# Attention's value products on two column tiles of 64 queries, 66 columns streamed in place of 128

## The chip, the cores and the metric

The kernel runs on one core of a Trainium2 chip. The metric is the device time of the whole program in microseconds (us). The kernel before was timed three times: 4877.83, 4884.79 and 4883.42 us, median 4883.42 us. One execution was profiled; its trace has a span of 4877.6 us from the first to the last instruction.

## What is computed

Two graph attention layers over x of shape (8, 2048, 256), with an adjacency matrix of 2048 x 2048. The change is in the first layer, whose core is this (float32, four heads of 64, keys in chunks of 256):

```python
h = jnp.maximum(_layernorm(x, axis=-1), 0.0)
q = (x @ Wq.T + bq).reshape(B, N, H, Dh).transpose(0, 2, 1, 3)     # k, v alike; here x is h
scores = jnp.einsum('bhnd,bhjcd->bhnjc', q, kc) / jnp.sqrt(jnp.asarray(Dh, dtype=q.dtype))
scores = jnp.clip(scores, -10.0, 10.0)
scores = jnp.where(mask == 0, jnp.asarray(-10.0, scores.dtype), scores)
attn = jax.nn.softmax(scores, axis=-1)          # over the 256 keys of a chunk
ctx = jnp.einsum('bhnjc,bhjcd->bhnd', attn, vc) # summed over the chunks j
ctx = ctx.transpose(0, 2, 1, 3).reshape(B, N, Dout)
out = ctx @ Wo.T + bo
out = out + x
out = (out - mu) * jax.lax.rsqrt(var + EPS) * gamma + beta
```

The softmax is taken within each chunk of 256 keys, so every chunk and head has its own denominator. The second layer (additive attention over all 2048 nodes, then elu) is not touched.

## The kernel before

The first layer goes through the 8 batches in one loop; batches 1 to 6 are one loop body. A batch is cut into 4 strips of 512 queries (STRIP), and a strip into 32 steps: 8 chunks of keys (c) times 4 heads (h). So there are 8 x 4 x 32 = 1024 steps. One step does this:

- TensorE, `scores`: for each half r of the chunk (128 keys) a product of keys (stationary, 128 x 128) with 512 queries, twice (L637 and L638, the high and the low part of the queries), into one of three PSUM slots. Four matmuls of 512 columns.
- ScalarE (ACT), L785: exp over the slot, 128 x 1024.
- VectorE (DVE), L921: clips by `bound`, which carries the mask, and writes `probs` in SBUF, keys on the partitions, 512 queries along the row. That frees the slot.
- TensorE, `values`: for each quarter q of the strip (128 queries) and each half r of the chunk one product. The stationary operand is `probs` (128 keys x 128 queries); the moving operand is `v_s` (128 keys x values). The result stands in the PSUM tile `outs`, 128 queries on the partitions. The values of head h are 64 columns of `v_s` followed by a column of ones (E1 = 65 columns per head), so column 64 of the result is the softmax's denominator. The kernel streams 128 columns from there, 63 more than are read afterwards. Eight products of float32, each of which the chip executes as two weight loads and two matmuls, so 16 of each per step in the trace.
- VectorE: the reciprocal of column 64 (L927), and a scaled sum into `ctx_sum` (L941, four per step, or L935 for the first chunk).

The order is written out by hand. On TensorE, step i issues `scores(s, i)` and then `values(s, i - LAG)` with LAG = 2, and in some steps a few more products between them: transposes of the next batch's strip (L559), queries of the next strip (L587), the turned context (L598) and the output projection (L610). After the last strip of a batch come the keys (L568) and values (L579) of the next batch. VectorE handles step i - 3's result before it clips step i. A value product waits on `slot_free` (its probabilities were written) and on `ctx_scaled` (its `outs` tile was read).

Of the kernel before, what the change touches and what calls it, by code (L numbers as in the profile page):

```python
# [28 lines left out]
P = 128  # L29
B, N, F = 8, 2048, 256  # L30
H, D = 4, 64
E1 = D + 1
CHUNK = 256
NC = N // CHUNK
JC = CHUNK // P
NT = N // P
# [39 lines left out]
PROBS = 4  # L76
LAG = 2
OUTS = 2
# [79 lines left out]
class Both:  # L158

    def __init__(self, nc, ctx):  # L160
        sb = lambda name, shape: ctx.enter_context(nc.sbuf_tensor(name, shape, F32))
        self.wide_s = sb("wide_s", [P, KC * F])
        self.w_s = sb("w_s", [P, KC * WIDE])
        self.x_s = sb("x_q_s", [P, NT * 2 * E1 + 2 * IT * F])
        self.h_s = sb("h_q_s", [P, 2 * NT * 2 * E1])
        self.t_s = sb("t_o_s", [P, KC * N])
# [7 lines left out]
def layer0_block(nc, x, adj, wq_t, bq, wk_t, bk, wv_t, bv, wo_t, bo, gamma, beta, w, a, x1, mask_dram, s_dram, d_dram, both):  # L174
    with ExitStack() as ctx:
# [30 lines left out]
        x1_in = both.t_s[:, :].rearrange("p (t f) -> p t f", t=NT)  # L206
        q_near = both.x_s[:, 0:NT * 2 * E1].rearrange("p (t h e) -> p t h e", t=NT, h=2)
        q_far = both.h_s[:, 0:NT * 2 * E1].rearrange("p (t h e) -> p t h e", t=NT, h=2)
        h1_t = both.h_s[:, NT * 2 * E1:NT * 2 * E1 + KC * 2 * P].rearrange("p (c n) -> p c n", c=KC)
        sd, d_max = both.sd, both.d_max  # L210
# [6 lines left out]

        k_hl = sb("k_hl", [P, H, N], F32R)
        q_hl = sb("q_hl", [P, H, 2, STRIP], F32R)
        v_w = H * E1 + P - E1  # L220
        v_s = sb("v_s", [P, NT, v_w])
        bound = sb("bound", [P, 2, JC, STRIP])
        probs = sb("probs", [P, PROBS, JC, STRIP])
# [9 lines left out]
        outs = [ps(f"outs{k}", [P, IT, P]) for k in range(OUTS)]  # L233
# [54 lines left out]
        def used(b, kind, *name):  # L288

            place = USES[kind][name]  # L290
            skipped = 2
            if kind == FIRST:
                skipped = sum(place >= USES[kind][(gone, 0)] for gone in ("turn", "project"))
            return b * BATCH_USES + PROLOGUE_USES - skipped + place

        def spot(kind, *name):

            return slots[used(0, kind, *name) % SLOTS]

        def q_used(b, kind, s, qu):  # L300

            if s > 0:
                return used(b, kind, "q", s, qu)
            if kind == FIRST:
                return q_first(qu)
            return used(b, MIDDLE, "q", 0, qu) - BATCH_USES
# [225 lines left out]
        def _(pe):  # L532
# [15 lines left out]
            def fill(u):  # L548
                pe.wait_ge(slot_free, u + 1)

            def freed(u):
                pe.wait_ge(slot_free, u + SLOTS + 1)
# [39 lines left out]
            def turn(g, use, slot):  # L592

                pe.wait_ge(ctx_scaled, OUTS + (g + 1) * STEPS)
                fill(use)
                for c in range(KC):
                    for q in range(IT):
                        last = nc.tensor.transpose(slot[:, c, q * P:(q + 1) * P],  # L598
                                                   ctx_sum[:, q, 2 * c:2 * c + 2, :].rearrange("p h d -> p (h d)"),
                                                   ident[:, :])  # L600
                last.then_inc(slot_filled, 1)

            def project(turned, use, slot):

                fill(use)
                freed(turned)
                for q in range(IT):
                    out = slot[:, q // 2, (q % 2) * F:(q % 2 + 1) * F]
                    for c in range(KC):
                        last = nc.tensor.matmul(out, ctx_t[:, c, q * P:(q + 1) * P], wo_s[:, c, :],  # L610
                                                start=(c == 0), stop=(c == KC - 1))
                last.then_inc(slot_filled, 1)
# [12 lines left out]
            def batch(b, kind):  # L625
                first, last = kind == FIRST, kind == LAST

                def scores(s, i):
                    c, h = divmod(i, H)
                    slot = spot(kind, "step", s, i)  # L630
                    if i % 2 == 0 and i < H:
                        freed(q_used(b, kind, s, i // 2))
                        pe.wait_ge(q_copied[i // 2], (b * NS + s + 1) * 2 * 16)
                    fill(used(b, kind, "step", s, i))
                    for r in range(JC):
                        kt = k_hl[:, h, (c * JC + r) * P:(c * JC + r + 1) * P]
                        nc.tensor.matmul(slot[:, r, :], kt, q_hl[:, h, 0, :], start=True, stop=False)  # L637
                        end = nc.tensor.matmul(slot[:, r, :], kt, q_hl[:, h, 1, :], start=False, stop=True)  # L638
                    end.then_inc(slot_filled, 1)

                def values(s, i):
                    c, h = divmod(i, H)
                    freed(used(b, kind, "step", s, i))

                    pe.wait_ge(ctx_scaled, (b * NS + s) * STEPS + i + 1)
                    for q in range(IT):
                        for r in range(JC):
                            end = nc.tensor.matmul(outs[i % OUTS][:, q, :], probs[:, i % PROBS, r, q * P:(q + 1) * P],  # L648
                                                   v_s[:, c * JC + r, h * E1:h * E1 + P],
                                                   start=(r == 0), stop=(r == JC - 1))  # L650
                    end.then_inc(probs_used, 1)

                for s in range(NS):
                    has_before = s > 0 or not first
                    for i in range(STEPS + LAG):
                        if i == TURN_AT and has_before:
                            turn(b * NS + s - 1, used(b, kind, "turn", s), spot(kind, "turn", s))
                        if i == W_AT and has_before:
                            project(used(b, kind, "turn", s), used(b, kind, "project", s), spot(kind, "project", s))
                        if i < STEPS and not (i == 0 and s > 0):  # L660
                            scores(s, i)
                        if i == STEPS + LAG - 1 and s < NS - 1:
                            scores(s + 1, 0)
                        if i in t_pairs(s) and not last:
                            strip, pair = t_pairs(s)[i]
                            order = strip + 1 if strip < NS - 1 else 0
                            src = ahead if strip == NS - 1 else hs[:, tiles(strip), :]
                            transposes(src[:, 2 * pair:2 * pair + 2, :], T_USES * (b + 1) + 2 * order + pair + 1,
                                       used(b, kind, "t", strip, pair), spot(kind, "t", strip, pair))
                        if i in Q_AT and s < NS - 1:  # L670
                            qu = Q_AT.index(i)
                            queries(s + 1, qu, used(b, kind, "q", s + 1, qu), spot(kind, "q", s + 1, qu))
                        if i in T1_AT and s == NS - 1 and last:
                            pair = T1_AT.index(i)
                            transposes(ahead[:, pair % 2 * 2:pair % 2 * 2 + 2, :], T_USES * B + pair + 1,
                                       used(b, kind, "t1", pair), spot(kind, "t1", pair))
                        if i in P1_AT and s == NS - 1 and last:
                            pair = P1_AT.index(i)
                            project1(used(b, kind, "t1", pair), used(b, kind, "p1", pair), spot(kind, "p1", pair))
                        if STEPS - 1 <= i < STEPS - 1 + Q_USES:  # L680
                            qu = i - (STEPS - 1)
                            if s == NS - 1 and not last:
                                keys(0, qu, used(b, kind, "t", 0, 1), used(b, kind, "k", 0, qu), spot(kind, "k", 0, qu))
                        if i >= LAG:
                            values(s, i - LAG)
                if not last:
                    for s, hp in k_order()[H // 2:]:
                        keys(s, hp, used(b, kind, "t", s, 1), used(b, kind, "k", s, hp), spot(kind, "k", s, hp))
                    for k in range(V_USES):
                        make_values(k, used(b, kind, "v", k), spot(kind, "v", k))  # L690
                        if k in Q_AFTER_V:
                            qu = Q_AFTER_V.index(k)
                            queries(0, qu, used(b, kind, "q", 0, qu), spot(kind, "q", 0, qu))
# [1187 lines left out]
```

## Time and profile before

| | |
|---|---|
| timed runs, median | 4883.42 us (4877.83 to 4884.79) |
| span of the profiled execution | 4877.6 us |
| lowest timed run less that span | 0.2 us |
| TensorE matmuls (PE) | 4739.8 us, 97% of the span |
| weight loads (PEld, beside PE) | 4347.8 us, 89% |
| VectorE (DVE) | 4078.2 us, 84% |
| ScalarE (ACT) | 2977.2 us, 61% |
| value products L648 | 16384 matmuls, 1988.3 us busy |
| score products L637, L638 | 4096 matmuls, 1697.9 us busy |

Busy time counts the union of the records of an engine. A matmul's record runs from its start to the modelled end of its last result, so successive matmuls overlap: 16 records of 275 ns take less than 16 x 275 ns. The distance from start to start is what a matmul costs in a sequence. The first layer's steps run from 88 us to about 3376 us; the second layer fills the rest. PEld is the loading of a stationary operand into the array, and it overlaps the matmul before it.

### The profile page before, as it was taken

To read this page: it belongs to the slowest core of one execution; us is meant where nothing else is said; L and a number is where in the kernel's file an instruction comes from. 1 tells how busy PE (TensorE), PEld (TensorE's weight loads), DVE (VectorE), ACT (ScalarE), POOL (GpSimd) and SP (SyncE) were. 2 spreads that over 40 slices of the span, in tenths; PEclk is the share of its full clock that TensorE was granted. 3 is DMA by queue.
4 is the path that set the end of the run, shared out by engine and by line. 5 is a ranking of instruction groups with operands and counts; after the bars stand their busy time and mean duration, and the time that the engine had idled before them with its cause. 6 is when DMAs were issued, how large, how long until landed. Compare 5 with 4: busy or idle time off the path is not lost. (4 is left out here: it accounts for less than half of the span.)

```text
span 4877.6 us, 136121 instructions
## 1 busy us (share of the span) xinstructions
PE 4739.8 (97%) x56349; PEld 4347.8 (89%) x56349; DVE 4078.2 (84%) x9728; ACT 2977.2 (61%) x3317; POOL 738.5 (15%) x613
## 2 busy tenths in 40 slices
PE   7999999999999999999999999997899999999999
PEld 5998899898899988989888998996899999999998
DVE  5888788787788877878877887787899999999999
ACT  5444444444444444444444444443899999999998
POOL 3121121111121211211211211011000110100100
PEclk9999999999999999999999999999999999999999
DMA  5100100001010001000001000010321221221221
GB/s 113 53 18 18 31 27 19 23 18 27 19 31 18 18 23 27 27 15 27 20 17 32 27 18 18 21 36 22 105 79 31 76 79 31 76 79 31 76 66 38
DMA packets 173916, 186.82 MB, mean 38 GB/s; under 512 B 7520, under 2 KB 157408, under 8 KB 173152
## 3 DMA queue, kind: packets, MB, share of 16 engines
q1 hardware_dynamic: 166192, 159.49, 11.9%
q0 software_dynamic: 7088, 18.36, 1.6%
q8 instruction: 459, 7.52, 0.6%
q14 instruction: 177, 1.45, 0.1%
HBM read 110.43 MB, written 38.03 MB: 30 GB/s over the span
## 5 line engine op out<-in xcount | busy, mean ns | idle before, releaser
L785 ACT ACTIVATE slot<-slot,shift 128x1024 f32<-128x1024 f32 x1024 | 1113.5, 1088 | 1568.7 <-PE slot L638 1568.7
L648 PEld LDWEIGHTS outs<-v_s,probs 128*128 128x128 f32 x16384 | 1974.5, 192 | 106.3 <-issue 29.7
L648 PE MATMUL outs<-v_s,probs 128*128 128x128 f32 x16384 | 1988.3, 275 | 0.0
L921 DVE SCALAR_TENSOR_TENSOR probs<-slot,bound 128x1024 f32<-128x1024 f32 x1024 | 1250.3, 1223 | 368.9 <-ACT slot L785 365.3
L1555 ACT ACTIVATE u<-s_all,d_sign 128x1024 bf16<-128x1024 f32 x1024 | 1117.1, 1138 | 56.9 <-PE sums L1456 39.5
L637 PE MATMUL slot<-q_hl,k_hl 128*128 128x512 f32 x2048 | 895.2, 437 | 18.5 <-DVE probs L921 9.9
L638 PE MATMUL slot<-q_hl,k_hl 128*128 128x512 f32 x2048 | 802.7, 392 | 0.0
L941 DVE SCALAR_TENSOR_TENSOR ctx_sum<-outs,inv,ctx_sum 128x64 f32<-128x64 f32 x3584 | 770.0, 278 | 31.7
L1452 PE MATMUL sums<-x_mixed,u 128*128 128x130 f16 x8192 | 785.5, 219 | 3.7 <-issue 3.5
L1456 PE MATMUL sums<-x_mixed,mask 128*128 128x65 f16 x8192 | 759.4, 193 | 5.5 <-issue 5.5
L1687 DVE TENSOR_TENSOR u<-u,mask 128x1024 f16<-128x1024 bf16 x1024 | 694.3, 689 | 76.6 <-ACT u L1555 67.6
L1447 PE MATMUL sums<-x_plain,u 128*128 128x65 f16 x16384 | 607.7, 194 | 59.1 <-DVE u L1696 54.1
L1456 PEld LDWEIGHTS sums<-x_mixed,mask 128*128 128x128 f16 x8192 | 640.6, 98 | 6.7 <-issue 6.5
L1447 PEld LDWEIGHTS sums<-x_plain,u 128*128 128x128 f16 x16384 | 561.8, 98 | 70.8 <-issue 41.4
L1452 PEld LDWEIGHTS sums<-x_mixed,u 128*128 128x128 f16 x8192 | 534.4, 97 | 17.9 <-issue 4.4
L637 PEld LDWEIGHTS slot<-q_hl,k_hl 128*128 128x128 f32 x2048 | 388.2, 190 | 72.1 <-DVE probs L921 20.6
L638 PEld LDWEIGHTS slot<-q_hl,k_hl 128*128 128x128 f32 x2048 | 388.5, 190 | 44.8
L1696 DVE TENSOR_TENSOR u<-mask,u 128x1024 f16<-128x1024 f16 x512 | 354.6, 693 | 0.0
L747 ACT ACTIVATE bound<-mask,low 128x1024 f32<-128x1024 uint8 x256 | 292.0, 1141 | 0.8
L481 POOL TENSOR_TENSOR y_rstd<-y_moments,eps_s 128x4 f32<-128x4 f32 x32 | 6.4, 201 | 1504.8 <-DVE y_moments L908 1504.8
L927 DVE RECIPROCAL inv<-outs 128x4 f32<-128x4 f32 x1024 | 176.7, 173 | 52.6 <-PE outs L648 50.8
L1380 POOL TENSOR_TENSOR mean_neg<-moments,neg_one 128x4 f32<-128x4 f32 x28 | 35.3, 1261 | 1099.1 <-DVE moments L1624 1099.1
(156 smaller groups left out, 3678.5 us busy)
## 6 DMA issues: line engine op xcount, KB each, us to landing
q_hl<-q_hl SPq DMA_DIRECT2D x128, 256.0 KB, 3.7
s_all<-s_turned SPq DMA_DIRECT2D x64, 512.0 KB, 5.7
x_q_s<-in_x SPq DMA_DIRECT2D x32, 512.0 KB, 4.6
x<-y SPq DMA_DIRECT2D x32, 512.0 KB, 3.2
t_o_s<-x SPq DMA_DIRECT2D x16, 1024.0 KB, 5.5
out<-t_o_s SPq DMA_DIRECT2D x16, 1024.0 KB, 6.9
x_q_s<-x SPq DMA_DIRECT2D x28, 512.0 KB, 5.8
probs<-in_adj POOLq DMA_DIRECT2D x12, 512.0 KB, 8.4
```

What stands on the lines that cost most here:

```text
L637: nc.tensor.matmul(slot[:, r, :], kt, q_hl[:, h, 0, :], start=True, stop=False)
L638: end = nc.tensor.matmul(slot[:, r, :], kt, q_hl[:, h, 1, :], start=False, stop=True)
L648: end = nc.tensor.matmul(outs[i % OUTS][:, q, :], probs[:, i % PROBS, r, q * P:(q + 1) * P], v_s[:, c * JC + r, h * E1:h * E1 + P], start= ...
L785: nc.scalar.activation(slot[:, :, :], slot[:, :, :], ACT.Exp, bias=shift[:, 0:1], scale=SCALE).then_inc(act_done, 1)
L921: nc.vector.scalar_tensor_tensor(probs[:, i % PROBS, :, :], spot(kind, "step", s, i)[:, :, :], P_LOW, bound[:, (i // H) % 2, :, :], ALU.ma ...
L941: op = nc.vector.scalar_tensor_tensor(ctx_sum[:, q, h, :], outs[i % OUTS][:, q, 0:D], inv[:, i % 2, q:q + 1], ctx_sum[:, q, h, :], ALU.mul ...
L1447: last = nc.tensor.matmul(group[:, side * E1:(side + 1) * E1], left, x_plain[:, h, j // 2, part, :], start=(j == 0 and t % PER_BANK == 0 a ...
L1452: nc.tensor.matmul(group[:, :], u[:, n % RING, cols], x_mixed[:, h, j // 2, 2 * part:2 * part + 2, :].rearrange("p k e -> p (k e)"), start ...
L1456: last = nc.tensor.matmul(group[:, E1:SUM_W], mask16[:, j, i0 + t * P:i0 + (t + 1) * P], x_mixed[:, h, j // 2, 4 + part, :], start=False, ...
L1555: nc.scalar.activation(cond[:, n % RING, :], s_all[:, m % HALVES, :], ACT.Relu, bias=d_sign[:, j, h:h + 1], scale=SIGN_SCALE).then_inc(con ...
L1687: nc.vector.tensor_tensor(u[:, n % RING, :], cond[:, n % RING, :], mask16[:, j, first:first + HALF], ALU.min).then_inc(u_made, 1)
L1696: nc.vector.tensor_tensor(u2[:, n // 2 % RESTS, :], mask16[:, j, first:first + HALF], u[:, n % RING, :], ALU.subtract).then_inc(u2_ready, 1)
```

## The change

Each value product over 128 queries becomes two over 64 queries. The first writes partitions 0 to 63 of `outs`, the second partitions 64 to 127; in the built program they have a tile size of 128 x 64, at column position 0 and at column position 64 of the array, where all else around them has 128 x 128. Each streams 66 columns of `v_s` (V_COLS: 64 values, the ones, and one more column that is not read). The padding of `v_s` shrinks with it, from 323 to 261 columns per tile of keys. Nothing else is changed; VectorE reads the same places of `outs`.

```diff
+V_COLS = E1 + 1
...
-        v_w = H * E1 + P - E1
+        v_w = H * E1 + V_COLS - E1
         v_s = sb("v_s", [P, NT, v_w])
...
                     for q in range(IT):
                         for r in range(JC):
-                            end = nc.tensor.matmul(outs[i % OUTS][:, q, :], probs[:, i % PROBS, r, q * P:(q + 1) * P],
-                                                   v_s[:, c * JC + r, h * E1:h * E1 + P],
-                                                   start=(r == 0), stop=(r == JC - 1))
+                            for g in range(2):
+                                rows_of = slice(g * D, (g + 1) * D)
+                                end = nc.tensor.matmul(outs[i % OUTS][rows_of, q, 0:V_COLS],
+                                                       probs[:, i % PROBS, r, q * P + g * D:q * P + (g + 1) * D],
+                                                       v_s[:, c * JC + r, h * E1:h * E1 + V_COLS],
+                                                       start=(r == 0), stop=(r == JC - 1))
                     end.then_inc(probs_used, 1)
```

On TensorE, in the first strip, this is what stands in the instruction order of the kernel before. The names are the tiles written and read, and "128x128" is the stationary operand's columns by the streamed ones:

```order
L648 MATMUL outs<-v_s,probs 128x128 [waits ctx_scaled,slot_free]
L648 MATMUL outs<-v_s,probs 128x128 x7
L637 MATMUL slot<-q_hl,k_hl 128x512 [waits slot_free]
L638 MATMUL slot<-q_hl,k_hl 128x512
L637 MATMUL slot<-q_hl,k_hl 128x512
L638 MATMUL slot<-q_hl,k_hl 128x512
L648 MATMUL outs<-v_s,probs 128x128 [waits ctx_scaled,slot_free]
L648 MATMUL outs<-v_s,probs 128x128 x7
```

And this stands there in the changed kernel, whose lines after L217 are one higher and whose value products are L651:

```order
L651 MATMUL outs<-v_s,probs 64x66 [waits ctx_scaled,slot_free]
L651 MATMUL outs<-v_s,probs 64x66 x15
L638 MATMUL slot<-q_hl,k_hl 128x512 [waits slot_free]
L639 MATMUL slot<-q_hl,k_hl 128x512
L638 MATMUL slot<-q_hl,k_hl 128x512
L639 MATMUL slot<-q_hl,k_hl 128x512
L651 MATMUL outs<-v_s,probs 64x66 [waits ctx_scaled,slot_free]
L651 MATMUL outs<-v_s,probs 64x66 x15
```

Eight products of a step became sixteen (so 32 weight loads and 32 matmuls at execution); the score products, the waits and their places are the same. The order on the other engines is as before.

## Rows read from the trace of the kernel before

**Rows 1.** The page: busy times, and the granted clock in 40 slices.
```profile
PE 4739.8 (97%) x56349; PEld 4347.8 (89%) x56349; DVE 4078.2 (84%) x9728; ACT 2977.2 (61%) x3317; POOL 738.5 (15%) x613
PEclk9999999999999999999999999999999999999999
```

**Rows 2.** Busy by stretch: length, PE, PEld, DVE, ACT, POOL, clock, DMA.
```profile
30.00:40.00 10.00, 5.26 (x33) 5.23 (x34) 7.87 (x11) 2.18 (x3) 5.87 (x8) 0.69 0.73 138
...
1834.80:1930.90 96.10, 95.78 (x684) 87.30 (x682) 78.62 (x211) 46.15 (x44) 19.26 (x15) 1.00 0.09 23
...
1740.40:2154.80 414.40, 410.70 (x2816) 367.34 (x2816) 333.72 (x876) 195.29 (x192) 77.02 (x60) 1.00 0.08 23
```

**Rows 3.** Waits in batch 4, 1740.4 to 2154.8 us: in total, times, longest.
```profile
ACT slot L785 <- PE slot L638: 196.7, 127, 5.1
...
DVE probs L921 <- ACT slot L785: 44.8, 88, 3.2
```

**Rows 4.** Timeline of matmuls in one step: start us, length us, what.
```profile
2000.54 1.95 PE L648 MATMUL outs<-v_s,probs 128*128 128x128 f32 x16
2002.24 0.48 PE L637 MATMUL slot<-q_hl,k_hl 128*128 128x512 f32 x1
2002.56 0.40 PE L638 MATMUL slot<-q_hl,k_hl 128*128 128x512 f32 x1
2002.79 0.39 PE L637 MATMUL slot<-q_hl,k_hl 128*128 128x512 f32 x1
2003.03 0.39 PE L638 MATMUL slot<-q_hl,k_hl 128*128 128x512 f32 x1
2003.25 0.27 PE L648 MATMUL outs<-v_s,probs 128*128 128x128 f32 x1
```

**Rows 5.** Timeline of weight loads in the same step.
```profile
2000.32 1.98 PEld L648 LDWEIGHTS outs<-v_s,probs 128*128 128x128 f32 x16
2002.22 0.19 PEld L637 LDWEIGHTS slot<-q_hl,k_hl 128*128 128x128 f32 x1
2002.33 0.19 PEld L638 LDWEIGHTS slot<-q_hl,k_hl 128*128 128x128 f32 x1
```

**Rows 6.** Groups of matmuls by shape: busy us, mean ns.
```profile
L648 PE MATMUL outs<-v_s,probs 128*128 128x128 f32 x16384 | 1988.3, 275 | 0.0
...
L587 PE MATMUL slot<-t_o_s,wide_s 128*128 128x512 f32 x256 | 120.3, 592 | 0.0
...
L579 PE MATMUL slot<-wv_s,t_o_s 128*128 128x256 f32 x512 | 115.1, 379 | 0.0
```

**Rows 7.** Groups of weight loads by shape.
```profile
L648 PEld LDWEIGHTS outs<-v_s,probs 128*128 128x128 f32 x16384 | 1974.5, 192 | 106.3 <-issue 29.7 <-DVE ctx_sum L941 2.9
...
L598 PEld LDWEIGHTS slot<-ident,ctx_sum 128*128 128x128 f32 x256 | 28.0, 141 | 19.8 <-issue 13.5 <-DVE ctx_sum L941 5.4
...
L1423 PEld LDWEIGHTS pro<-ident,sd 128*16 128x16 f32 x28 | 2.5, 90 | 0.0
...
L719 PEld LDWEIGHTS slot<-ident,sd 128*64 128x64 f32 x1 | 0.1, 113 | 0.0
```

**Rows 8.** Timeline of matmuls in layer two, around one 16-column stationary operand.
```profile
3485.83 0.23 PE L1456 MATMUL sums<-x_mixed,mask 128*128 128x65 f16 x2
3485.90 0.27 PE L1423 MATMUL pro<-ident,sd 128*16 128x128 f32 x1
3486.01 0.48 PE L1447 MATMUL sums<-x_plain,u 128*128 128x65 f16 x10
```

**Rows 9.** Groups on VectorE in batch 4.
```profile
L921 DVE SCALAR_TENSOR_TENSOR probs<-slot,bound 128x1024 f32<-128x1024 f32 x128 | 156.3, 1223 | 45.3 <-ACT slot L785 44.8 <-issue 0.3
L941 DVE SCALAR_TENSOR_TENSOR ctx_sum<-outs,inv,ctx_sum 128x64 f32<-128x64 f32 x448 | 96.2, 278 | 4.0
L927 DVE RECIPROCAL inv<-outs 128x4 f32<-128x4 f32 x128 | 22.1, 173 | 6.0 <-PE outs L648 5.8
```

## The prediction

> **What bounds the kernel now.** I read the page's busy times first: PE is busy for 97% of the span, VectorE for 84%, at a clock of nine tenths or more of full speed in all slices [rows 1]. That does not say which of the two ends last, so I took the first layer apart by stretches. In one strip of 96.10 us PE is busy for 95.78 us and VectorE for 78.62 us; in a whole batch of 414.40 us it is 410.70 and 333.72 us [rows 2]. The waits agree: ScalarE waits 196.7 us of the batch for score products, VectorE 44.8 us for exp [rows 3], and TensorE waits for nearly nothing. So the first layer goes at the pace of TensorE, and every nanosecond added to its steps is added to the time, 1024 times. A nanosecond taken away counts only until VectorE is the slower one.
>
> Then one step. The value products start at 2000.54 and the next step's at 2003.25, so a step takes 2.71 us [rows 4]. Sixteen value matmuls span 1.95 us with the last one's 275 ns [rows 4, 6], so they start every (1950 - 275) / 15 = 111.7 ns. What limits that? Two things that cost the same. Streaming: 512 columns last 592 ns and 256 last 379 ns [rows 6], so a float32 column streams in 213 / 256 = 0.832 ns and 128 take 106.5 ns. Loading: a load of 16 columns lasts 90 ns, one of 64 lasts 113 and one of 128 lasts 141 [rows 7]; that is 0.455 ns a column on a fixed 83 ns, for transposes. The value products' own load of 128 float32 columns lasts 192 ns [rows 7], so (192 - 83) / 128 = 0.85 ns a column, 109 ns in all. The order of the two is a lock step: the score product's load begins at 2002.22, when the last value matmul has begun, and the next load begins at 2002.33 [rows 5], 110 ns on, when the product that used the first could begin. One load runs under one matmul, and about 5 ns are lost at each change.
>
> **The change part by part.** Removed per step: 16 matmuls of 128 columns and 16 loads of 128. Added: 32 of 66 columns and 32 loads of 64. Streaming falls not by half but grows: 32 x 66 = 2112 columns for 16 x 128 = 2048. Loading stays: 32 x 64 is 2048 columns too. So halving the stream gives nothing unless the two column tiles work at the same time; that is the whole question.
>
> - The pitch of one half, if matmuls come one after another: 66 x 0.832 = 54.9 ns of streaming, 64 x 0.85 = 54.4 ns of loading under it, and the 5.2 ns of today's pitch (111.7 less 106.5) for the change of hands: 60.1 ns.
> - The end of the run of values: the next score product loads 128 columns, which take 109 ns. Today a 106.5 ns matmul covers that load. After the change the last value matmul streams for 54.9 ns, so from its start to the score product's pass 111.7 ns, not 60.1. The score load has lost half its cover.
> - Sum for a step: before 16 x 111.7 = 1787 ns. After 31 x 60.1 + 111.7 = 1975 ns. That is 188 ns more, and 1024 x 0.188 = 192 us.
> - The start of the run is free: the first value load, now 54.4 ns, lies under a score product that takes 230 ns to the next start [rows 4].
> - VectorE, ScalarE and POOL do what they did. Their slack covers 188 ns a step, since VectorE is idle for (96.10 - 78.62) / 32 = 546 ns of one [rows 2]. The smaller fill of v_s with ones is at the start, while the first loads of x are on their way; I cost it at nothing, and it was one instruction.
> - The clock: PE stays as busy as it was, so I leave it at full speed. The row in which it was not, 30 to 40 us at 0.69 of full clock, has PE busy for 5.26 us of 10 [rows 2].
>
> No row of before shows two column tiles in turn. The bounds for the pitch of a half: above, load and stream laid end to end with the change of hands, 54.4 + 54.9 + 5.2 = 114.5 ns, a step of 32 x 114.5 = 3664 ns, +1.88 us a step. Below, both tiles wholly at once, 60.1 ns for two halves, 30 ns each, -0.77 us a step, of which VectorE lets only a part through (below). I take 60.1 because the nearest row, the lock step of today's value products, shows that each load waits for the matmul before it to start and each matmul for its load. If that holds across tiles, loads alone make it 54.4 + 5.2 = 59.6 ns, even if the streams could overlap.
>
> A change of the array's tiling. In the second layer the transposition L1423 has a stationary operand of 16 columns, which the built program places on a tile of 128 x 32, between neighbours of 128 x 128. It starts at 3485.90 and its follower at 3486.01 [rows 8]: 110 ns, which is what its 128 columns need to stream (106.5). The matmul before it is no further away either: two of 65 columns start from 3485.83 on. So going there and back costs nothing to be seen, 28 times. I cost the 2048 changes of the new kernel at nothing. The Trainium skill's page "TensorEngine Tiling (Array Packing)", section "Tiling Modes", says the opposite: changing the mode drains TensorE. The trace does not bear that out for these 28; by the rule there would be two drains in every step, the third rival below.
>
> The sum against the profiled execution: its span of 4877.6 us and some 0.2 us around it, plus 192, is 5070 us. The median of the three timed runs lies 5.6 us above that execution, so against the median it is 5075 us, which I take.
>
> **The rivals.**
>
> First, the tiles work side by side. Then the second half of one product loads and streams beside the first half, matmuls still starting in program order; of four passes (two a half) two adjacent ones overlap, so 16 x 60.1 = 0.96 us for the values. PE would need 0.96 + 0.05 (the bare score load) + 0.92 for the scores, 1.93 us a step, and VectorE is the bound. Its three groups take (156.3 + 96.2 + 22.1) / 128 = 2.15 us a step [rows 9]. For a whole batch: 414.40 - 4 x 96.10 = 30 us are projections on PE and stay. In the other 384 us VectorE works for about 4 x 78.62 = 314, so at most 70 us go, 560 in all (4318) [rows 2]. Some waits come back, as VectorE now has a chain PE, ScalarE, VectorE that must be always ready; I take 55 us a batch, 440 in all: 4440 us, 4390 to 4520. For it: different tiles share no weights and no result partitions, so nothing in the data forbids it. Against: in no row does a load begin ahead of the start of the matmul before it. The Trainium skill's "TensorEngine Tiling (Array Packing)", section "Key Properties" under "Tiling Modes", says that different tiles can run loads and matmuls in parallel; no run so far shows that. What could spoil it is the clock, if PE is idle for a fifth of each step; the only loaded stretch with such a drop had PE idle for half.
>
> Second, nearly no change. The halves alternate between tiles, so the 5.2 ns of handing over vanish under the other tile's stream, and only the loads count: 32 x 54.4 + 54.6 = 1795 ns, 8 ns more than now, +8 us. With 1 ns less or more for a half this is 32 ns a step, 33 us. 4850 to 4930 us, middle 4891.
>
> Third, on the far side: TensorE empties at each change of tiling. A matmul's record of 275 ns less 106.5 ns of streaming leaves 168 ns until its last result is out [rows 6]; twice a step that is 336 ns, 344 us over 1024 steps, on top of 192: 5419 us. It decides once a drain costs more than the 20 ns that would be visible. Rows 8 speak against it, but with one tile position only, and never with the second tile at column 64. The end-to-end bound (+1.88 us a step, 6800 us) belongs here too and has nothing for it but that the case was never seen.
>
> **How the numbers follow.** Forecast 0.40 (5030 to 5100), side by side 0.35, nearly no change 0.13, drains or worse 0.12. A change of 0.2%, 10 us, is about what a measurement of this kernel can tell. Faster: 0.35 and 0.05 of the second rival, 0.40. Within 0.2%: 0.04 of it. Slower: 0.40 + 0.04 + 0.12 = 0.56. The likeliest is 5075 us, alone 5030 to 5100. The cases lie on both sides, so the range is wide: 4400 (the first rival without its last tenth) to 5110, leaving out the drains and the tails.
>
> **What would show it.** A step's length, 2.71 us now, should read 2.90 in the timeline. The 32 value matmuls should start every 60 ns, their run from the first one to the score product's real start last 1.98 us, of which the last 112 ns are one load. The group's mean should be 275 - 62 x 0.832 = 223 ns, the load's 137. VectorE's share should fall, its wait for exp grow. If the halves' starts come in close pairs (4 to 30 ns apart and then a gap), the tiles overlap, the step is near 2.2 us and TensorE's waits for `slot_free` and `ctx_scaled` appear: I am wrong on the sign. If a gap of more than 100 ns stands between the last 512-column matmul and the first value matmul, beyond its 230 ns, it is the drain.

## The result and the profile after

The changed kernel takes 4494.94 us (median of four runs, 4492.85 to 4499.48), against 4883.88 us before in the same comparison: a ratio of 0.9207, with a 95% interval of 0.9194 to 0.922. It is 389 us faster where I had forecast 192 us slower. The first rival, two tiles that work side by side, is what happened, and at 4440 us it promised somewhat more than came.

The page of the changed kernel, with the lines that answer to [rows 1, 6, 7]:

```profile
PE 4246.6 (95%) x72733; PEld 3492.7 (78%) x72733; DVE 4024.7 (90%) x9728; ACT 2977.8 (66%) x3317; POOL 714.7 (16%) x613
...
PEclk9999999999999999999999999989999999999999
...
L651 PEld LDWEIGHTS outs<-v_s,probs 128*64 128x64 f32 x32768 | 1042.2, 137 | 450.5 <-issue 271.3
...
L651 PE MATMUL outs<-v_s,probs 128*64 128x66 f32 x32768 | 1179.5, 225 | 62.7 <-DVE ctx_sum L945 58.1
```

One value matmul lasts 225 ns and one load 137 ns, as predicted (223 and 137): what a half costs alone was right. But 32768 of them make 1179.5 us of busy time where 16384 made 1988.3 [rows 6]. The timeline of one step shows how (start us, length us, what), first the matmuls, then the weight loads:

```profile
1660.23 0.40 PE L638 MATMUL slot<-q_hl,k_hl 128*128 128x512 f32 x1
1660.46 0.40 PE L639 MATMUL slot<-q_hl,k_hl 128*128 128x512 f32 x1
1660.79 1.15 PE L651 MATMUL outs<-v_s,probs 128*64 128x66 f32 x32
1661.87 0.50 PE L638 MATMUL slot<-q_hl,k_hl 128*128 128x512 f32 x1
```

```profile
1660.78 1.01 PEld L651 LDWEIGHTS outs<-v_s,probs 128*64 128x64 f32 x32 [0.37 <-DVE ctx_sum L945]
1661.87 0.19 PEld L638 LDWEIGHTS slot<-q_hl,k_hl 128*128 128x128 f32 x1
1661.98 0.19 PEld L639 LDWEIGHTS slot<-q_hl,k_hl 128*128 128x128 f32 x1
```

The 32 matmuls span 1.15 us where 16 took 1.95 us [rows 4]. Cut down to 15 ns at the start of the run, the same timeline has two of them:

```profile
1660.79 0.28 PE L651 MATMUL outs<-v_s,probs 128*64 128x66 f32 x2
```

Two matmuls within 0.28 us, of which each alone is 0.27 us long: they start 7 ns apart. Their loads start 7 ns apart too. The last record is 0.222 us long, and the first one begins with a load that nothing covers (0.05 us). Without these two the 16 pairs have a pitch of (1.15 - 0.27) / 15 = 0.059 us by these rounded figures, and 58.3 ns by the starts in the trace. That is about the pitch I expected of one half; it is that of two.

The second thing to see is what stands around the run. Before, the first load of the values began 3 ns after the last score product had started. Now it begins 0.32 us after (1660.46 to 1660.78), although score products in a row start every 0.23 us: some 0.095 us are lost. At the end the last value matmul starts at 1661.72 (1660.79 + 1.15 - 0.22), and the score product's load follows 0.15 us later, where 66 columns stream for 0.055 us: again 0.095 us are lost. The trace puts the first of these gaps down to VectorE (`ctx_sum`); the experiments show that this is the wrong name in a plain step.

The step's median fell from 2.709 to 2.214 us, and TensorE is still back to back in it: 0.93 (scores) + 0.93 (values) + 0.35 (two stalls of 0.095 us, and the loads that they lay bare, about 0.10 us for a score product and 0.05 us for a value product). By stretches, with the columns of [rows 2], a strip and a batch:

```profile
1630.90:1714.70 83.80, 80.33 (x1192) 60.22 (x1192) 76.75 (x211) 46.16 (x44) 19.25 (x15) 1.00 0.10 27
1547.30:1911.60 364.30, 348.31 (x4864) 259.25 (x4865) 326.77 (x877) 195.34 (x192) 77.05 (x60) 1.00 0.10 27
```

A strip went from 96.10 to 83.80 us, 12.3 us less. 32 plain steps would give 32 x 0.495 = 15.8 us. Most of the rest is in steps in which VectorE has a side job: its work is 76.75 us of the 83.80, and such steps last 2.3 to 3.0 us. Of the 1023 distances between steps in the first layer, 598 are under 2.25 us. Another part is at the turn of a strip: its last two steps take 10.97 us together where they took 10.65 (means over 18 strips). There TensorE now waits for a DMA that brings the next strip's queries, 2.9 us in the whole kernel before and 35.9 us now:

```profile
L637 PE MATMUL slot<-q_hl,k_hl 128*128 128x512 f32 x2048 | 895.2, 437 | 18.5 <-DVE probs L921 9.9 <-DVE v_s L865 4.8 <-DMA q_hl<-q_hl 2.9
L638 PE MATMUL slot<-q_hl,k_hl 128*128 128x512 f32 x2048 | 919.7, 449 | 59.1 <-DMA q_hl<-q_hl 35.9
```

The first line is of the kernel before, the second of the changed one; the last figures are the idle time of TensorE before these products, and what ended it.

### The profile page after: what moved, and what is told of

The parts are those of the page before. It is cut to its first block and busy times, and to the rows that moved or that the text cites. A ratio compares the mean times of both kernels' runs of the same rounds, so it can differ in the third digit from the quotient of the medians.

```text
span 4491.0 us, 168889 instructions
## 1 busy us (share of the span) xinstructions
PE 4246.6 (95%) x72733; PEld 3492.7 (78%) x72733; DVE 4024.7 (90%) x9728; ACT 2977.8 (66%) x3317; POOL 714.7 (16%) x613
## 5 line engine op out<-in xcount | busy, mean ns | idle before, releaser
L651 PEld LDWEIGHTS outs<-v_s,probs 128*64 128x64 f32 x32768 | 1042.2, 137 | 450.5 <-issue 271.3
L651 PE MATMUL outs<-v_s,probs 128*64 128x66 f32 x32768 | 1179.5, 225 | 62.7 <-DVE ctx_sum L945 58.1
L638 PE MATMUL slot<-q_hl,k_hl 128*128 128x512 f32 x2048 | 919.7, 449 | 59.1 <-DMA q_hl<-q_hl 35.9
L639 PE MATMUL slot<-q_hl,k_hl 128*128 128x512 f32 x2048 | 812.6, 397 | 0.0
L1460 PE MATMUL sums<-x_mixed,mask 128*128 128x65 f16 x8192 | 759.2, 193 | 4.6 <-issue 4.5
L1460 PEld LDWEIGHTS sums<-x_mixed,mask 128*128 128x128 f16 x8192 | 640.6, 98 | 5.9 <-issue 5.9
L1384 POOL TENSOR_TENSOR mean_neg<-moments,neg_one 128x4 f32<-128x4 f32 x28 | 21.7, 774 | 1123.2 <-DVE moments L1628 1123.2
```

Of the source, the lines that this page charges most:

```text
L651: end = nc.tensor.matmul(outs[i % OUTS][rows_of, q, 0:V_COLS], probs[:, i % PROBS, r, q * P + g * D:q * P + (g + 1) * D], v_s[:, c * JC + ...
L1460: last = nc.tensor.matmul(group[:, E1:SUM_W], mask16[:, j, i0 + t * P:i0 + (t + 1) * P], x_mixed[:, h, j // 2, 4 + part, :], start=False, ...
```

## The experiments

All start from the changed kernel; the ratios are to the kernel before, which ran beside them.

**e1_untiled66: is it just the narrower stream?**

```diff
-                            for g in range(2):
-                                rows_of = slice(g * D, (g + 1) * D)
-                                end = nc.tensor.matmul(outs[i % OUTS][rows_of, q, 0:V_COLS], ...
+                            end = nc.tensor.matmul(outs[i % OUTS][:, q, 0:V_COLS], probs[:, i % PROBS, r, q * P:(q + 1) * P],
...
```

> The value products stay on the whole array (128 queries stationary, 16 matmuls and 16 loads a step) and stream 66 columns. Theory A (the two column tiles work side by side, and today's pitch is held up by the weight load as much as by the stream): the loads of 128 float32 columns take 109 ns each, so the pitch stays 110 to 112 ns and the time stays at 4870 to 4890 us. Theory B (the gain of the change is just the narrower stream; loads are not a bound): the pitch falls to about 60 ns, the step to 1.9 to 2.2 us and the time to 4350 to 4500 us.

4891.94 us, ratio 1.0023 (1.0012 to 1.0033). From its timeline:

```profile
1662.43 0.39 PE L639 MATMUL slot<-q_hl,k_hl 128*128 128x512 f32 x1
1662.66 1.89 PE L649 MATMUL outs<-v_s,probs 128*128 128x66 f32 x16
1664.36 0.48 PE L638 MATMUL slot<-q_hl,k_hl 128*128 128x512 f32 x1
```

Half of the stream taken away, and sixteen matmuls still take 1.89 us. The load of 128 columns (192 ns long, by the prediction's estimate 109 ns of occupation) holds the pitch by itself: value matmuls start every 111.7 ns here and in the kernel before alike. Theory A holds, and B falls. The small loss fits the step of the prediction on lost cover: the score product's load now begins 54 ns after the last value matmul, which covers only half of it; a step is 2.716 us.

**e2_tiled128: two tiles, wide streams**

```diff
-V_COLS = E1 + 1
+V_COLS = P
```

> Two column tiles of 64 queries as in the change, but each streams 128 columns, so 4096 columns a step in place of 2112. Theory A (side by side): the starts come in pairs 7 ns apart, a pair every 110 to 112 ns as with one matmul of before, and the step is that of before plus the two stalls of about 148 ns at the changes between the score and the value products: 2.71 + 0.30 = 3.0 us, 5180 us. Theory C (the tiles only take turns, and the change gained by something else, such as the smaller loads): the streams add up, 32 x 111.7 = 3.57 us for the values, step 4.5 us, 6700 us.

5183.98 us, ratio 1.0623 (1.0605 to 1.0641); expected 5180.

```profile
1661.58 0.39 PE L639 MATMUL slot<-q_hl,k_hl 128*128 128x512 f32 x1
1661.89 1.97 PE L651 MATMUL outs<-v_s,probs 128*64 128x128 f32 x32
```

32 matmuls of 128 columns take as long as 16 did before (1.97 and 1.95 us). A pair starts every 109.2 ns, where 128 columns need 106.5. So streams on different column tiles overlap fully, and the narrow stream and the two tiles are each worth nothing alone: the first leaves the load as the bound, the second the stream. Together they halve the run. The difference from the kernel before, 303 us, is 1024 times the 0.30 us of the two stalls.

**e3_blocked: one tile after the other**

```diff
-                    for q in range(IT):
-                        for r in range(JC):
-                            for g in range(2):
+                    for g in range(2):
+                        for q in range(IT):
+                            for r in range(JC):
```

> The same 32 matmuls a step as the change, in another order: all 16 on the tile of queries 0 to 63 first, then all 16 on the other tile. Theory A with starts in program order: a matmul can run beside another only if its neighbour in the order is on the other tile, so nothing overlaps; the pitch is the 60 ns that I predicted for one after another, the values take 1.92 us, and the step is 0.93 + 1.92 + 0.05 + 0.30 = 3.2 us, 5350 us. Rival (each tile has a queue of its own that runs ahead): like the change, 4495 us.

5109.54 us, ratio 1.0473 (1.0456 to 1.049); expected 5350 or 4495.

```profile
1900.51 0.39 PE L639 MATMUL slot<-q_hl,k_hl 128*128 128x512 f32 x1
1900.83 1.90 PE L651 MATMUL outs<-v_s,probs 128*64 128x66 f32 x32
1902.66 0.50 PE L638 MATMUL slot<-q_hl,k_hl 128*128 128x512 f32 x1
```

The same instructions in another order lose the overlap: 1.90 us for the run. My number was too high for two reasons. On one tile the pitch is 58.3 ns, not 60. And the theory's "nothing overlaps" was too strict: in the middle of each run three matmuls start 1 to 6 ns after another, so some of the other tile's start while the first tile's last ones are still to come, and about 0.18 us of the run overlap (31 x 58.3 = 1.81 us, against 1.90 - 0.27 = 1.63). So a few matmuls can be passed over, not sixteen: neighbours in the order should be on different tiles. This is also the closest measurement of my forecast's assumption, and of its sign. That its time lies near my 5075 us is in part luck: it has 0.30 us of stalls a step that I had left out, and the overlap and the shorter pitch take most of that back.

**e4_tile0_only: is the second tile free?**

```diff
-                            for g in range(2):
+                            for g in range(2 if first and s == 0 and i < OUTS else 1):
```

> Leaves out the value products of queries 64 to 127 of each 128 (all but those of the first two steps), so half of the value products' work is gone; all else stays. Theory A: the other tile's work ran for free beside this one's, so the pitch stays at 58 ns for 16 matmuls, the run at 0.93 us and the time at 4495 us. Rival (the tiles share the load path or issue, and a pair's 58 ns are the sum of two parts): the pitch falls towards 30 ns and the run to 0.5 us; the step then goes to what VectorE needs, 2.15 us, about 4430 us. It also tells whether the stalls of about 148 ns at both ends of the run need the second tile at column 64: if yes, the first matmul of the run starts 230 ns after the last score product and not 326 ns plus a load.

4502.77 us, ratio 0.9224 (0.9208 to 0.9239).

```profile
1662.01 0.40 PE L639 MATMUL slot<-q_hl,k_hl 128*128 128x512 f32 x1
1662.33 1.15 PE L651 MATMUL outs<-v_s,probs 128*64 128x66 f32 x16
1663.41 0.50 PE L638 MATMUL slot<-q_hl,k_hl 128*128 128x512 f32 x1
```

Sixteen matmuls take the 1.15 us of thirty-two. The second tile's work is free, and the stalls are there without it.

**e5_pairs and e6_more_switches: are the gaps stalls of the tiling or waits for VectorE?**

e5 issues two steps' scores, then two steps' values:

```diff
-                        if i >= LAG:
+                        if i >= STEPS:
+                            values(s, i - LAG)
+                        elif i % 2 and i > LAG:
+                            values(s, i - LAG - 1)
                             values(s, i - LAG)
```

> The changed kernel, with TensorE's order in pairs: the score products of steps i and i+1, then the value products of steps i-2 and i-1, so half as many changes between the whole array and the 64-column tiles (steps after the last score product stay as they were). Theory D (each change empties the array and costs about 148 ns to the next real start, two per step): PE needs 2.07 us a step in place of 2.21, below VectorE's 2.15 us, so the step goes to about 2.15 to 2.18 us and the time to 4430 to 4470 us, and two of three long starts of 325 and 150 ns become starts at the normal pitch. Rival (the gaps at the changes are waits for ctx_sum or for the slots, which pairs don't shorten): 4490 us or more.

e6 splits both functions in two and alternates the parts:

```diff
...
+                        split = LAG <= i < STEPS
+                        if split:
+                            scores(s, i, 0)
+                            values(s, i - LAG, 0)
+                            scores(s, i, 1)
...
+                            values(s, i - LAG, 1 if split else None)
```

> The changed kernel with twice the changes of tiling and the same products: in steps 2 to 31 of a strip the order is scores of half r=0, half of the values, scores of r=1, the other half of the values. Theory D: 2 more changes of 148 ns in 30 of 32 steps, PE-bound throughout, so 2.21 + 0.30 = 2.51 us a step and 4495 + 284 = 4780 us. Rival (the gaps are waits on VectorE's results): 4500 us, or a rise without the 325 and 150 ns starts in the middle of a step.

e5: 4494.94 us, ratio 0.9212 (0.9198 to 0.9226). e6: 4808.63 us, ratio 0.9854 (0.9839 to 0.9869); expected 4780. The timeline of e5:

```profile
1661.58 0.39 PE L639 MATMUL slot<-q_hl,k_hl 128*128 128x512 f32 x1
1661.89 2.26 PE L651 MATMUL outs<-v_s,probs 128*64 128x66 f32 x64
1664.08 0.50 PE L638 MATMUL slot<-q_hl,k_hl 128*128 128x512 f32 x1
```

And that of e6:

```profile
1560.17 0.50 PE L639 MATMUL slot<-q_hl,k_hl 128*128 128x512 f32 x1
1560.51 0.40 PE L640 MATMUL slot<-q_hl,k_hl 128*128 128x512 f32 x1
1560.97 0.69 PE L653 MATMUL outs<-v_s,probs 128*64 128x66 f32 x16
1561.59 0.50 PE L639 MATMUL slot<-q_hl,k_hl 128*128 128x512 f32 x1
1561.93 0.39 PE L640 MATMUL slot<-q_hl,k_hl 128*128 128x512 f32 x1
...
1563.64 0.40 PE L640 MATMUL slot<-q_hl,k_hl 128*128 128x512 f32 x1
1563.97 0.69 PE L653 MATMUL outs<-v_s,probs 128*64 128x66 f32 x16
```

e6 is clear: twice the changes add 314 us to the 4495, and the gap stands in the middle of a step too. The second half of a step's values waits for no semaphore. Where nothing stands between it and the score product before it (832 times), it starts 327 ns after that one (median; all but one under 335 ns), just as the first half does. So the gap is not a wait for VectorE. e5 has half of the stalls. Two of its plain steps take 4.23 us, 2.12 a step in place of 2.21, but the whole kernel is not faster. Its strip:

```profile
1632.70:1717.00 84.30, 77.22 (x1192) 60.69 (x1192) 77.30 (x212) 45.24 (x44) 19.29 (x15) 1.00 0.10 27
```

TensorE has 3.1 us less to do than in the change, and the strip takes 84.3 us as before. In the plain steps VectorE is now the bound: its clips start every 2.11 us. What two plain steps gain, 0.20 us, is lost where VectorE has side jobs: steps 20 and 21 of a strip take 5.3 us together in e5 and 4.6 us in the change (means over 18 strips). My 2.15 us for VectorE had left the side jobs out; with them its work is 76.75 / 32 = 2.40 us a step. Theory D was right on the stall and wrong on the time. That VectorE's work over a whole strip holds the time is argued from this, e7 and e9; no run here isolates it.

**e7_half_products: how much is left on TensorE?**

```diff
-                        for r in range(JC):
+                        for r in range(1):
...
-                                                       start=(r == 0), stop=(r == JC - 1))
+                                                       start=True, stop=True)
```

> The changed kernel without the value products of the second half of each chunk (keys 128 to 255), so 16 of 32 matmuls a step are left out. If PE with its two stalls is still the bound of a step (2.21 us) and VectorE comes at about 2.15 us, PE falls to 1.75 us a step and the time to 4420 to 4460 us, no further: VectorE's floor. If VectorE is far from the bound, about 4050 us (0.47 us less in each of 1024 steps). If VectorE is the bound now, 4495 us as the change.

4447.10 us, ratio 0.9112 (0.9098 to 0.9126), in the first range. Its strip:

```profile
1608.46:1692.42 83.96, 69.10 (x681) 47.46 (x681) 76.35 (x210) 45.91 (x44) 19.22 (x15) 0.96 0.10 26
```

Eleven microseconds of TensorE's work are gone from this strip, and its length is unchanged; the whole kernel gains 48 us, of which 10 and 13 us in the first and the last batch. Two plain steps take 4.23 us, exactly as in e5, so 2.11 us is what VectorE needs in a plain step. With fewer products TensorE idles more and its clock is lower (0.96 here, 1.00 in the change's strip), so this floor is not wholly clean.

**e8_65_columns**

```diff
-V_COLS = E1 + 1
+V_COLS = E1
```

> The changed kernel with 65 columns streamed in place of 66. If the stream sets the pitch of a pair (58.3 ns), it falls by 0.83 ns, 13 ns a step, 14 us in all where PE is the bound: 4481 to 4490 us. If the weight loads (54.4 ns and a change of hands) set it, nothing changes: 4495 us. If an odd number of float32 columns costs extra, slower.

4495.05 us, ratio 0.921 (0.9198 to 0.9223), beside 0.9207 of the change. The pairs start every 58.3 ns in both traces, so the column less is worth nothing in the run: by the expectation's own rule the weight load sets that pitch, if only just. A plain step is 2.207 us in place of 2.213, but these few nanoseconds stand between two score products. An odd count costs nothing.

**e9_norm_on_pool and e10_pairs_norm_on_pool: is VectorE the bound where it has side jobs?**

```diff
                             if i == 17:
                                 inverse_std(b * NS + s + 2, tiles(s - 1))
+                                pool.wait_ge(rstd_done, b * NS + s + 2)
+                                pool_gate(nc, pool_cell)
+                                for t in range((s - 1) * IT, s * IT):
+                                    op = nc.gpsimd.tensor_scalar(hs[:, t, :], xs[:, t, :], moments[:, t, 0:1],
+                                                                 rstd[:, t:t + 1], ALU.subtract, ALU.mult)
+                                    if t % 2:
+                                        op.then_inc(norm_x_done, 1)
...
-                    if 22 <= i < 22 + IT:
-                        t = t0 + i - 22
-                        if i == 22:
-                            dve.wait_ge(rstd_done, b * NS + s + 2)
-                        op = normalize(hs[:, t, :], xs[:, t, :], t)
-                        if i % 2:
-                            op.then_inc(norm_x_done, 1)
```

> The changed kernel with four of VectorE's side jobs moved: in strips 1 to 3 of batches 0 to 6 (21 strips) the four normalizations of the next batch's rows, 0.455 us each on VectorE, are done by GpSimd, which is busy for 16%. Theory E (after the change VectorE is the bound in the steps that carry such a job, which last 2.3 to 2.7 us in place of 2.21): 0.9 to 1.8 us less per strip, 4457 to 4476 us. Rival (TensorE with its stalls is the bound everywhere): 4495 us. A second rival: GpSimd's work slows VectorE's, and the time rises.

> As e9_norm_on_pool, with TensorE's order in pairs as in e5_pairs, which by itself left the time at 4495 us though its plain steps went from 2.21 to 2.12 us. Theory E: with pairs VectorE is the bound everywhere, so all of 4 x 0.455 us counts in 21 strips, 38 us: 4457 us. If pairs are bound by something else at the ends of a strip: 4480 us or more.

e10 is the edits of e9 and e5 together. e9: 4468.92 us, ratio 0.9158 (0.9145 to 0.917), the fastest version here that computes everything. e10: 4471.41 us, ratio 0.9165 (0.9152 to 0.9177). In e9 three of the steps that lost their side job (24, 25 and 28 of a strip) went from 2.34, 2.43 and 2.67 us to 2.21 (medians over the strips), to the length of a plain step. So in such steps VectorE was the bound, and in plain ones TensorE. Pairs add nothing to that: e10 was expected at 4457 us, and of its two theories neither came out. As in e5, two plain steps take 4.23 us and steps 20 and 21 of a strip 5.3 us; what holds those steps in the order of pairs I did not isolate.

**e11_four_tiles**

```diff
+QT = 32
...
-                            for g in range(2):
-                                rows_of = slice(g * D, (g + 1) * D)
+                            for g in range(4):
+                                rows_of = slice(g * QT, (g + 1) * QT)
...
```

> The changed kernel with four column tiles of 32 queries in place of two of 64: 64 matmuls of 66 columns a step, each with a load of 32 columns. Theory A (tiles work side by side, the stream sets the pitch of a group): starts come in fours about 7 ns apart, a group every 58 ns, two passes a product as before, so the run stays 0.93 us and the time 4495 us. Rival (issue or loading is shared: 14.6 ns a matmul is near the floor of it): 64 matmuls take more than 0.93 us; at 25 ns each 1.6 us, 2.9 us a step, 5180 us.

4497.17 us, ratio 0.9216 (0.9202 to 0.923).

```profile
1661.50 0.40 PE L640 MATMUL slot<-q_hl,k_hl 128*128 128x512 f32 x1
1661.82 1.13 PE L652 MATMUL outs<-v_s,probs 128*32 128x66 f32 x64
1662.88 0.50 PE L639 MATMUL slot<-q_hl,k_hl 128*128 128x512 f32 x1
```

64 matmuls in 1.13 us: four tiles run side by side. With loads of 32 columns a group starts every 57.7 ns, which leaves the stream of 66 columns (54.9 ns) as what sets the pitch; the loads of 64 held it at 58.3. The run is 0.02 us shorter than the change's, and the time shows nothing of it. The stalls are the same.

**e12_turn_as_product: why [rows 8] showed no stall**

```diff
-                nc.tensor.transpose(bank(k, T_PAIRS + IT)[0:SD_ROWS, 0:P], ...
+                nc.tensor.matmul(bank(k, T_PAIRS + IT)[0:SD_ROWS, 0:P], ...
```

> The changed kernel with one operation of the second layer, 28 times executed, written as a product with the identity in place of a transposition. Its stationary operand of 16 columns stands on a tile of 128 x 32 in both, between neighbours of 128 x 128, and as a transposition it showed no stall: the weight load after it began 2 ns after its start. Theory F (only products on column tiles empty the array, a transposition is executed without leaving the whole array): the load of the product now begins after its neighbour's 27 ns stream and some 94 ns more, and the next load that much after its last stream (107 + 94 = 200 ns). Rival (the stall belongs to the neighbours, float32 in the first layer and float16 here): loads begin 2 ns after the matmul before, as with the transposition. The time tells nothing of 28 x 0.3 = 8 us.

One run, 4508.57 us; its time is not compared. Matmuls, then loads, in its timeline:

```profile
3110.73 0.23 PE L1460 MATMUL sums<-x_mixed,mask 128*128 128x65 f16 x2
3110.88 0.39 PE L1427 MATMUL pro<-ident,sd 128*16 128x128 f32 x2
3111.21 0.27 PE L1451 MATMUL sums<-x_plain,u 128*128 128x65 f16 x3
```

```profile
3110.88 0.11 PEld L1427 LDWEIGHTS pro<-ident,sd 128*16 128x16 f32 x2
3111.21 0.18 PEld L1451 LDWEIGHTS sums<-x_plain,u 128*128 128x128 f16 x4 [0.21 <-issue]
```

The last L1460 starts at 3110.76, and the load of L1427 now 0.12 us later; as a transposition it came 2 ns after. The second L1427 starts at 3111.00 (3110.88 + 0.39 - 0.27), the next load 0.20 us later, of which 0.107 us is its stream. All 28 are alike, 121 to 123 and 200 to 202 ns. The same tile between the same neighbours stalls as a product and not as a transposition. It is not the change from float16 to float32 either: in the same trace the float32 product L1420, on the whole array between float16 products, has its first load 1 to 2 ns after the matmul before it. Theory F holds in what it says of the stall. That a transposition is executed without leaving the whole array would explain it, but is not shown.

## Why the prediction was wrong

- **TensorE bounds the first layer, load and stream cost the same.** Right within 3 ns: loads of 128 columns give a pitch of 111.7 ns (e1), streams of 128 alone 109.2 ns (e2).
- **A half is 54.9 ns of streaming under 54.4 ns of loading.** Right: 58.3 ns with the change of hands (e3, e4), where I had 60.1.
- **Matmuls come one after another, since each load waits for the matmul before it and each matmul for its load.** This is the step that failed. The lock step of [rows 4, 5] is real, but all those matmuls used the whole array, so the row could not tell "the next matmul" from "the next matmul on this tile". The lock step holds within a tile (e3: 58.3 ns); between tiles loads and streams overlap (e2, e4, e11), so the 32 matmuls take 0.93 us from first to last start, and not the 31 x 60.1 = 1.86 us of my sum. I made the nearest row into a rule for a case in which its reason does not apply. The Trainium skill's "TensorEngine Tiling (Array Packing)", section "Key Properties", says that different tiles can load and multiply in parallel. The trace agrees, with pairs 7 ns apart.
- **The score product's load loses its cover at the end of the run.** Right in e1 (54 ns from the last value matmul to that load). In the change it is part of a larger loss.
- **Changing the tiling costs nothing.** This step failed too, by 0.30 us a step (e2). In the trace of the change the next load starts about 95 ns later than the last stream allows, whatever that was: 325 ns after a score product (230 to the next start in a row), 150 after a value matmul (55), 201 after the transposition L560 (107), 521 after the query projection L588 (512 float32 columns, 426). Where the tile stays the same, as from a score product to L588, it starts 2 or 3 ns after. Then the load lies bare, so a change costs 0.15 us in all. I read "nothing" from a transposition on a tile, which does not stall (e12). The third rival had the stall, and priced it at 0.336 us a step. That this is near the 0.30 is in part luck: it has TensorE wait 168 ns for the last result, and the trace shows 95 ns, with the bare loads for the rest. By the modelled ends the next load even starts before the last result is out (1661.87 against 1661.94), so that the array empties first is not shown. The sign that I had set for it, more than 100 ns beyond the 230, was missed by 3 ns. The same section of the Trainium skill says that changing the mode drains TensorE. The trace agrees that a change costs time, for products; it does not show what is drained.
- **The first rival's price.** I gave 440 us (55 a batch of the 70 that VectorE would leave); it was 389. A batch fell by 50 us. In it I had TensorE at 1.93 us a step, without stalls; it is 2.21, so TensorE with its stalls holds the plain steps and VectorE those with side jobs. e7, where TensorE has about 1.75 us of work a step, takes 4447 us, close to the rival's 4440; but nearly half of its gain is in the first and the last batch, so how the missing 51 us divide stays open. The rival also had nothing for the DMA of the queries, on which TensorE now waits 33 us longer than before.
- **The clock** fell to half in a few short stretches more than before, four of six after TensorE had waited 1.7 to 2.6 us at the turn of a strip. The columns are again those of [rows 2]:

```profile
330.00:340.80 10.80, 8.20 (x112) 5.44 (x110) 9.24 (x27) 5.22 (x7) 0.00 (x0) 1.00 0.33 74
340.80:344.20 3.40, 3.40 (x36) 2.67 (x35) 0.79 (x5) 1.09 (x1) 0.00 (x0) 0.50 0.23 77
```

Six such stretches of 3.4 to 6.8 us in the steps, 24 us together, cost at most 12 us by an estimate at half speed.

## What to carry to other kernels

In this kernel, where float32 products alternate with their weight loads, a run costs the larger of load and stream. Narrowing the stream alone or splitting the array alone gains nothing (e1, e2); halves of the stationary operand on two column tiles, issued alternately, with a stream no wider than needed, halve the run. Each move between whole-array products and column tiles costs 0.15 us, so it pays from runs well above that, and a run of tiled products should not be broken up. Before such a forecast ask whether the row from which a rule is read could have shown the other case at all; and once TensorE's share falls, look at the steps in which the next engine has side jobs, not at its mean.

## What I had not expected of the hardware

- Matmuls and loads on different column tiles start 7 ns apart and run fully side by side, two or four of them (e2, e11). A run of sixteen on one tile lets only the last few overlap with the other tile's first (e3).
- Entering and leaving a column tile of 64 or 32 columns stalls TensorE for about 95 ns beyond the last stream, after matmuls of 65 to 512 columns alike, for products of float32 and beside ones of float16. A transposition on such a tile does not stall (e12 against [rows 8]).
- The profile named VectorE as what the stall at the start of a run waited for. That was the wait whose semaphore came last before the load, not its cause: e6 has the same 327 ns where the products wait for no semaphore.
